# First chunk of a CIN layer on one Trainium2 core: shifted operand partly by selection matmuls instead of DRAM loads

## What is computed

```python
e  = stack([tbl_f[ids[:, f]] for f in range(39)], axis=1)       # (1024, 39, 16)
x1 = relu(einsum('bhd,bmd,shm->bsd', e,  e, W1) + b1)           # layer 1, (1024, 128, 16)
x2 = relu(einsum('bhd,bmd,shm->bsd', x1, e, W2) + b2)           # layer 2, (1024, 128, 16)
z  = concatenate([x1.sum(-1), x2.sum(-1)], axis=-1)             # (1024, 256)
h  = concatenate([z, dense_ctx], axis=1)
h  = maximum(h @ W_top1 + b_top1, 0); h = maximum(h @ W_top2 + b_top2, 0)
y  = h @ W_top3                                                 # (1024, 1)
```

## Time and profile before

| what | us |
|---|---|
| median of three runs | 1221.91 |
| profiled execution, its own time | 1218.08 |
| its span (first to last instruction) | 1216.3 |
| PE (matmul) busy in the span | 1130.8 (93%) |
| DVE busy | 941.1 (77%) |
| ACT busy | 801.2 (66%) |
| POOL busy | 847.9 (70%) |
| matmuls of layer 2, L604, three groups of 1280 | 542.3 + 498.1 + 475.5 (overlapping) |
| matmuls of layer 1, L588, 448 records | 233.1 |

### The profile page before, as it was taken

How to read it: one execution, slowest core, us unless ns; L and a number is a source line. 1 busy time by engine, 2 the same in 40 slices (tenths; PEclk the granted TensorE clock), 3 DMA queues, 4 the chain that set the end, 5 groups by cost and what they waited for, 6 DMA issues and landing times.

```text
span 1216.3 us, 17500 instructions
## 1 busy us (share of the span) xinstructions
PE 1130.8 (93%) x4468; PEld 829.6 (68%) x4468; DVE 941.1 (77%) x2846; ACT 801.2 (66%) x2718; POOL 847.9 (70%) x956
## 2 busy tenths in 40 slices
PE   0069999999999999999999999999999999999996
PEld 0037777777777777777776567777777777776685
DVE  2027878889898888888887468998888889875786
ACT  4017767777777767777776467777776777765683
POOL 7745878788678878778787466788777864542455
PEclk9999999999999999999999999999999999999997
DMA  5256568675876477665976248764686748652341
GB/s 167 46 124 142 106 127 178 127 150 103 177 164 126 93 149 170 137 131 100 202 139 139 46 81 178 163 137 82 146 174 122 141 99 200 148 129 44 71 92 33
DMA packets 73516, 154.47 MB, mean 127 GB/s; under 512 B 14339, under 2 KB 27525, under 8 KB 73414
## 3 DMA queue, kind: packets, MB, share of 16 engines
q0 software_dynamic: 28272, 85.81, 39.5%
q1 hardware_dynamic: 45142, 67.53, 21.0%
HBM read 66.26 MB, written 3.81 MB: 58 GB/s over the span
## 4 chain that ended last, share of the span: by engine, by line
PE 58%; issue 15%; POOL 14%; DMA 8%; DVE 2%; ACT 1%; SPq 1%; another core or an unknown queue 1%; POOLq 0%; DVEq 0%; ACTq 0%
PE bank L604 46%; PE l_acc L588 10%; DMA prod<-prod 6%; POOL tree L306 4%; POOL emb L277 2%; POOL tree L313 2%; POOL prod L288 2%; POOL tree L318 1%; POOL a_sum L327 1%; DVE acc L506 1%; DMA z<-e_rows 1%; ACT prod L394 1%; PE misc L624 1%; PE misc L627 1%
## 5 line engine op out<-in xcount | busy, mean ns | idle before, releaser
L394 ACT ACTIVATE prod<-bank,emb 128x128 f32<-128x128 f32 x2560 | 724.7, 376 | 329.3 <-PE bank L604 299.5
L506 DVE SCALAR_TENSOR_TENSOR acc<-bank,emb,acc 128x128 f32<-128x128 f32 x2176 | 612.5, 342 | 154.7 <-PE bank L604 133.6
L604 PE MATMUL bank<-w2h,x1h 128*128 128x512 f32 (+1 forms) x1280 | 542.3, 424 | 8.2 <-DVE acc L506 4.5
L604 PE MATMUL bank<-w2l,x1h 128*128 128x512 f32 (+1 forms) x1280 | 498.1, 389 | 0.0
L604 PE MATMUL bank<-w2h,x1l 128*128 128x512 f32 (+1 forms) x1280 | 475.5, 434 | 2.0 <-issue 1.5
L277 POOL DMA_INDIRECT emb<-tbl,idx x312 | 311.2, 997 | 82.2 <-issue 76.0
L604 PEld LDWEIGHTS bank<-w2h,x1h 128*128 128x128 f32 x1280 | 241.2, 188 | 113.2 <-issue 58.5
L306 POOL TENSOR_TENSOR tree<-prod 128x640 f32<-128x640 f32 x128 | 241.7, 1888 | 91.2 <-DMA prod<-prod 91.1
L604 PEld LDWEIGHTS bank<-w2h,x1l 128*128 128x128 f32 x1280 | 240.9, 188 | 92.8 <-issue 37.2
L604 PEld LDWEIGHTS bank<-w2l,x1h 128*128 128x128 f32 x1280 | 241.6, 189 | 67.9 <-issue 23.3
L288 POOL DMA_DIRECT2D prod<-prod x127 | 125.1, 985 | 184.8 <-ACT prod L394 182.0
(11 more groups left out here) (79 smaller groups left out, 291.3 us busy)
## 6 DMA issues: line engine op xcount, KB each, us to landing
prod<-prod POOLq DMA_DIRECT2D x127, 640.0 KB
z<-e_rows SPq DMA_DIRECT2D x160, 234.0 KB
z<-e_rows SPq DMA_DIRECT2D x192, 78.0 KB
emb<-tbl,idx POOLq DMA_INDIRECT x312
z<-e_rows SPq DMA_DIRECT2D x32, 156.0 KB
prod<-w_by_h SPq DMA_DIRECT2D x3, 832.0 KB
e_rows<-e_t SPq DMA_DIRECT2D x8, 256.0 KB
wt<-w_top SPq DMA_DIRECT2D x2, 512.0 KB
```

Source lines behind the costliest of these rows:

```text
L394: last = nc.scalar.activation(prod[:, ct % P_RING, i, n * S:(n + 1) * S], bank[:, (ct * NB + k) % RING, n * S:(n + 1) * S], ACT.Copy, scal ...
L506: nc.vector.scalar_tensor_tensor(dst, src, scale, dst if step else b2_row[:, :], ALU.mult, ALU.add).then_inc(v_step, 1)
L604: last = nc.tensor.matmul(out_bank[:, 0:b - a], x, w[:, a:b], start=(n == 0), stop=(n == 2))
```

## The change

For chunk 0 alone, the unshifted rows and K-tiles 0, 1 and 2 no longer come from DRAM. The four dimensions of chunk 0 are transposed from the gathered rows of tile 0 (39 fields x 128 samples each) into a PSUM bank; ScalarE copies the 39 x 512 block to `z[0:39, 0, 7, :]`; four float32 matmuls with constant 0/1 matrices `sel` (39 x 117) spread it to `e_rep` and to three PSUM banks, K-tiles 0 to 2. ScalarE copies `e_rep` to SBUF (`rep_copy`, in a slot of `prod`), because VectorE then multiplies that copy with a PSUM bank. K-tiles 3 to 6 of chunk 0 are loaded from `e_rows` as before; SyncE issues six loads for it where it issued twelve, and one more at the start for `sel` (73 KB). All other chunks are unchanged.

TensorE also gets matmuls whose results nobody reads: 16 (`WARM_LATE`) between `lift(0, 0)` and `lift(0, 1)`, and 8 (`WARM_X1`) after the last contraction of chunk 0. They have 512 columns and the operands of layer 2's kind (`w2h`). The first layer 2 bank waits for `x1h` before its first matmul and for `x1l` only before its third.

```diff
+SPREAD = 3
+WARM_LATE = 16
+WARM_X1 = 8
...
+def spread_rows():
+    sel = np.zeros((M, SPREAD + 1, KP * M), np.float32)
+    for s in range(SPREAD + 1):
+        for k in range(KP):
+            for h in range(M):
+                f = h if s == 0 else (h + KP * (s - 1) + k) % M
+                sel[f, s, k * M + h] = 1.0
+    return sel
...
+        rep_copy = prod[0:KP * M, 0, 0, :]
...
+            sp.dma_start(sel[:, :, :], dram["sel"]).then_inc(in_sel, 16)
...
-                for h in range(KP):
+                for h in range(KP if f else 0):
                     first = bass.AP(tensor=e_rows[tile % 2], offset=q * CH, ap=[[ROW, M], [1, CH]])
                     sp.dma_start(z[h * M:(h + 1) * M, r, NF, :], first).then_inc(in_rep[r], 16)
                 for k, ts in enumerate(Z_GROUPS):
-                    for h in range(KP):
+                    ts = [t for t in ts if f or t >= SPREAD]
+                    for h in range(KP if ts else 0):
...
             copy_lifted(0, 0)
             copy_lifted(0, 1)
-            copy_rep(0)
+            act.wait_ge(d0_turned, 1)
+            nc.scalar.copy(z[0:M, 0, NF, :], bank[0:M, SPREAD, :]).then_inc(d0_ready, 1)
+            act.wait_ge(rep_ready, 1)
+            act.wait_ge(w2l_made, NB)
+            nc.scalar.copy(rep_copy, e_rep[0:KP * M, :]).then_inc(rep_copied, 1)
...
                 dve.wait_ge(rep_ready, f + 1)
+                if f == 0 and t < SPREAD:
+                    dve.wait_ge(rep_copied, 1)
+                    dve.wait_ge(spread, t + 1)
+                    nc.vector.tensor_tensor(z[0:rows, 0, t, :], rep_copy[0:rows, :], bank[0:rows, t, :], ALU.mult
+                                            ).then_inc(f_made, 1)
+                    return
...
-                    pe.wait_ge(x1l_done, c + 1)
+                        pe.wait_ge(x1h_done, 1)
+                    else:
+                        pe.wait_ge(x1l_done, c + 1)
...
+                    if ct == 0 and k == 0 and n == 2:
+                        pe.wait_ge(x1l_done, 1)
...
+            def warm(n):
+                for _ in range(n):
+                    nc.tensor.matmul(bank[:, 4, :], w2h[:, 0:P], w2h[:, 0:CH], start=True, stop=True)
+
+            def spread_first():
+                for d in range(DC):
+                    turned = emb[:, 0, :].rearrange("p (f d) -> p d f", d=D)[:, d, :]
+                    last = nc.tensor.transpose(bank[0:M, SPREAD, d * P:(d + 1) * P], turned, ident_f[:, :])
+                last.then_inc(d0_turned, 1)
+                pe.wait_ge(in_sel, 16)
+                pe.wait_ge(d0_ready, 1)
+                nc.tensor.matmul(e_rep[0:KP * M, :], sel[:, 0, :], z[0:M, 0, NF, :], start=True, stop=True
+                                 ).then_inc(rep_ready, 1)
+                for t in range(SPREAD):
+                    nc.tensor.matmul(bank[0:KP * M, t, :], sel[:, t + 1, :], z[0:M, 0, NF, :], start=True, stop=True
+                                     ).then_inc(spread, 1)
+
+            pe.wait_ge(w2l_made, NB)
+            pe.wait_ge(w1_summed, 1)
             lift(0, 0)
+            warm(WARM_LATE)
             lift(0, 1)
+            spread_first()
...
+                        if f == 0 and g == CONTRACT_AT[-1]:
+                            warm(WARM_X1)
```

More of the change, by code:

```diff
@@ L121, in build @@
         y = sb("y", [1, B])
+        sel = sb("sel", [M, SPREAD + 1, KP * M])
         w2_f = prod[:, :, :, :].rearrange("p r a n -> p (r a n)")[:, 0:M * S]
+        rep_copy = prod[0:KP * M, 0, 0, :]
         w1_back = tree[:, :, :].rearrange("p r n -> p (r n)")[:, 0:NF * S]
@@ L147, in build @@
         w2h_cast, w2_staged, w2l_made = sem("w2h_cast"), sem("w2_staged"), sem("w2l_made")
+        in_sel, d0_turned, d0_ready, spread = sem("in_sel"), sem("d0_turned"), sem("d0_ready"), sem("spread")
+        rep_copied = sem("rep_copied")
         lifted, et_ready, rep_ready = sem("lifted"), sem("et_ready"), sem("rep_ready")
@@ L374, in copy_rep @@
             def copy_rep(f):
-                act.wait_ge(in_rep[f % 2], 48 * (f // 2 + 1))
+                act.wait_ge(in_rep[f % 2], 48 * (f // 2 + f % 2))
                 wait(act, f_made, NF * f)
@@ L462, in make_f @@
                 dve.wait_ge(rep_ready, f + 1)
+                if f == 0 and t < SPREAD:
[4 more added lines that the diff above has]
+                    return
                 for k, ts in enumerate(Z_GROUPS):
-                    if t == ts[0]:
-                        dve.wait_ge(in_z[f % 2][k], 48 * (f // 2 + 1))
+                    if t == ts[0] or (f == 0 and t == SPREAD and t in ts):
+                        loads = f // 2 + (0 if f % 2 == 0 and k == 0 else 1)
+                        dve.wait_ge(in_z[f % 2][k], 48 * loads)
                 nc.vector.tensor_tensor(z[0:rows, f % 2, t, :], e_rep[0:rows, :], z[0:rows, f % 2, t, :], ALU.mult
@@ L700 @@
         "ident": load("ident_const", np.eye(P, dtype=np.float32)),
+        "sel": load("spread_const", spread_rows()),
         "w1_ahead": load("w1_ahead", ahead),
```

## The result

The changed kernel takes **1239.87 us** (median of 5 runs, 1238.89 to 1241.26) against 1221.91 us: a ratio of 1.0141, 95% interval 1.0122 to 1.0160. It is slower by 18 us, and the forecast was 8.4 us faster. The profiled execution took 1240.37 us with a span of 1238.6 us.

What follows compares the result with a forecast made beforehand. PE bounds the kernel from 92 to 1190 us, so an earlier stream start is an earlier end. 1218.08 - 8.4 = 1209.7 us profiled; with the median 3.8 above that, 1213.5 us, range 1204.5 to 1219.8.

Steps and rivals of the forecast that it cites:

- Cost zero; the cover is the wait for the gathers: Sixteen spare matmuls between the lifts: 6.9 us from 45.2 to 52.1, ahead of 53.06; up to 6.9 us if uncovered.
- rival 3: Hand-overs from PE are what is slow: five late by 4 us each is 20 us, about 1233 us; chance 0.05.
- the odd SyncE: Nine prologue loads take 11.08 and 11.20 us to issue, 1.2 us apiece; the first three take 1.12 us together.
- the 8.4 us: Gain at the stream's start: SyncE's slow issuing of chunk 1's loads ends earlier by six fewer loads at 1.4 us.
- What bounds the kernel: From 92 us to 1190 us PE is the bound, 249.76 of 250 us busy; an earlier stream start is an earlier end.
- The condition that I had put: An earlier stream start ends the kernel earlier as long as GpSimd, the gathers and the loads aren't late for it.
- The slow stretch: Around layer 2's start: DVE's first bank at 88.34 after 10.02 us of waiting, and slow SyncE issues; cause not named.
- All three values: Gain by how that stretch ends: same length 6.8 us, with SyncE's slow issuing 8.4 us (taken), vanishing 14.2 us.
- The prologue's sum: Transposes, selections, loads and contractions before layer 2: contractions end at 68.0 against 74.35, layer 2 starts 6.8 us earlier, about 71.0.
- The 1.36 us between contraction and ReLU: ReLU at 75.71 ran 1.36 us after PE's end; forecast to stay.
- rival 2: The clock doesn't come up in the prologue: chain end 74.1, 1219 to 1221 us; chance 0.2.
- Loads, copy_rep(1), POOL's slack: Chunk 0's loads there at 63.1; copy_rep(1) done at 66.1, hidden by 1.9 us; POOL may come 17 us late.

Runs made afterwards that it cites:

- paced versions: Changed kernel, tile 1's gathers held, then spread, no spares: 1216.15 us; five at once, others later and slower: 1210.13 us, or 1212.79 us with 8 spares.
- paced version without spares: Changed kernel without spares, five of tile 1's gathers at once, others held until the seventh product, then 3.4 per quarter chunk: 1210.13 us.

## Why the prediction was wrong

**The step that failed** is the first of the change: "Cost zero; the cover is the wait for the gathers", for the 16 spare matmuls. Their time on PE was covered, as costed. What I had put at nothing, and what the runs showed, is that spare instructions of PE beside a dense row of gathers put back the updates that PE posts after them: the second lift's reader ran 25.1 us late with them and within 0.1 us without, and with them alone in the kernel before the copy came at 78.37. It came out as rival 3, which I gave 0.05 and a price of 4 us a hand-over; the two that were hit cost 25.1 and 9.5 us more, and the later ones nothing, since the gathers were then over. My argument against it, that ACT took PE's result within 0.1 us at 53.56, was true of a PE that had issued ten instructions by then, and the change gave it 32 more. I had named the two signs, PE's late results and the odd SyncE, and taken them for one stretch that *ends* at some time; I didn't ask what PE and GpSimd did ahead of them.

**A second step failed beside it**: the 8.4 us by which the selections and the fewer loads were to bring the stream forward. With no spares at all the change still gave 1223.98 us and not 1213.5. The contractions' update was 11.9 us late there, and DVE's first layer 2 step came at 92.80, 4.5 us later than in the kernel before. The term itself was also mis-sized by its own rows: the six loads that go are three that took 1.12 us together and three of the nine that took 11.08 us, some 4.8 us and not six times 1.4.

**What bounds the kernel** was right for the change: PE is the bound behind the start, and the changed kernel ends later because it starts later. The condition that I had put, that GpSimd and the gathers aren't late, is what the paced versions broke: of 14.3 us by which DVE's first step came forward without spares 3.1 were left at the end.

**The slow stretch.** All three values were wrong for this kernel, since it is not a stretch with a length. It ends at 88.2 in the changed kernel, at 88.4 and 88.5 without spares and at 88.3 before, whatever starts when: some 9 us after the last of the 61 first gathers was issued (to 79 us). SyncE shows the same instant: its issues are of 0.70 us or twice that up to 88.1 and of 0.37 us from 88.14 on in the changed kernel, and change over at 88.3 in the kernel before. The last packets of the gathers had run by 80.1 and 80.9 us in these two, so what ends at 88 is not the gathers' own transfers. With the gathers held until 76.73 it moved with them (issued to 103.9 us, ACT late up to 107.89), and with them spread no such stretch is left.

**The prologue's sum**, which the changed kernel couldn't show, can be read from the paced version without spares. Transposes 1.06 us (1.09 forecast), `e_rep` from 54.90 (55.0), contractions from 61.97 (61.8), their end at 70.14 (68.0), layer 2 at 71.60 (71.0). The contraction was off by 2.1 us because the clock rose later than I took it: its weight loads are 0.86 us apart up to 65.55 and 0.43 us from 66.11 on. In the changed kernel the selections and contractions of 88.9 to 99.5 us all ran at 1.2 GHz, in an unbroken row, and then at 2.4:

```profile
88.90:99.50 10.60, 10.60 (x12) 3.82 (x13) 4.45 (x7) 0.74 (x2) 0.00 (x0) 0.50 0.52 136
99.60:104.00 4.40, 4.40 (x12) 2.00 (x11) 0.00 (x0) 0.33 (x1) 0.00 (x0) 1.00 0.00 0
```

The 1.36 us between contraction and ReLU was no fixed cost but the same lateness; it was 0.04 us in the paced version.

**The clock, rival 2**, came true beside it: the spares did raise the clock (the lift took 0.32 us, not 0.46) and it was down again long before it was of use. The Trainium skill ("TensorE: Matmul & The Clock Gate", Part 4: PE-mode transpose) says that transposes don't count as activity; this trace doesn't test it: the granted clock was 0.53 over the 24.6 us after them, but PE stood idle all that time.

**Loads, copy_rep(1), POOL's slack** played no part in the changed kernel: `copy_rep(1)` was done 4.1 us ahead of ReLU. In the paced versions GpSimd became what was late, which I had looked for in `prod` and not in the lift of tile 1.

## What to carry to other kernels

Work whose results nobody reads is not free because its engine is idle: here it also put back that engine's completions, by 25 us and more. Where one engine's wait is booked on nothing and the writer's row ended long before, look at what else posts then (here 61 gathers in a row), take instructions away from the writer or traffic from the path, and try that first. And put a burst that is wanted late (tile 1's rows, first read at 161 us in the kernel before) where nothing waits for short hand-overs, at a pace that its engine can hold.

## What the runs showed of the hardware

While gathers are issued every 1.25 us, the update at the end of a matmul reached ACT 25.1 us late and the next one 34.5 us late, although the matmuls themselves ran on time; ACT's own updates were in time in the same stretch (its copy ended at 78.63 and SyncE stored at 78.66; in the kernel before x1h ended at 77.00 and DVE began at 77.03). Sixteen matmuls of 32 columns did as much harm to the next hand-over as sixteen of 512 (25.7 and 25.2 us); four of 512 did none to it. With the gathers held, the prologue's updates came within 0.1 us in the version without spares. In the kernel before a milder form of it (ACT 4.5 us late at 83.42, DVE 8.6 us at 88.34) had been there all along, and pacing the gathers alone gave 5 us. The lateness lasts some 8 us beyond the gathers' last packet (80.1 and 88.1 in the changed kernel).

Open: which part of a gather fills the path (its packets, its updates, GpSimd's writing of it), and whether the recording of the instructions for the profile takes part. All runs here were recorded in the same way, so none can show it. The number of PE's instructions is told apart from its columns and its clock, and from its busy time only in part (3.58 against 5.19 us). Gathers issued in another way weren't tried.
